# Decay attention: 22 instead of 26 tiles of maxima ahead of the first step, and each set of maxima sent in two transfers, the first ahead of the second group's packed rows

## The chip, the cores and the metric

The kernel runs on one core of one Trainium2 chip. The metric is the device time of one execution in microseconds. A core has TensorE (PE in the profile, its weight loads PEld), VectorE (DVE), ScalarE (ACT), GpSimd (POOL) and SyncE (SP), which here issues all DMAs.

## The reference, cut to what matters

The program is a chain of eight residual blocks on 2 batches of 1024 tokens by 128 features; the activation is kept transposed, 128 features on the partitions and 2048 tokens along the free axis, in chunks of 512. The change touches the fifth block alone, the decay attention, between two normalizations:

```
q = x @ W_q; k = x @ W_k; v = x @ W_v
latent_kv = (k + v) @ W_down_kv
k_rec, v_rec = latent_kv @ W_up_k, latent_kv @ W_up_v      # 16 heads of 8 features
scores = einsum('bhqd,bhkd->bhqk', qh, k_rec) / sqrt(128)
scores = scores * exp(-0.01 * |i - j|)                     # decay, before the softmax
out = einsum('bhqk,bhkd->bhqd', softmax(scores), v_rec)
x = x + out @ W_o
```

There are 2 batches of 16 heads, each with scores of 1024 x 1024. The softmax subtracts the exact row maximum, so that the maximum of each query's decayed scores has to be known before the exponential of that query is taken.

## The kernel before, in words

The heads go through in eight groups of four (n = 0 to 7; groups 0 to 3 are batch 0). For every group the queries and keys, split into bf16 pieces of 48 rows, are brought from a scratch tensor in HBM into packed rows in SBUF (`packs(n)`, L1290, eight transfers of 192 KB), with two more rows (KP and KP + 1) for the maxima.

Two kinds of work run over these rows.

*Maxima.* A unit `u` (256 in all, 32 in a group) is one head and 128 queries: TensorE makes 128 x 1024 scores (L916), VectorE multiplies them by the decay strip and takes the maximum in one instruction (`unit_dve`, L926). When the 16 units of half a group are done, a *turn* `j` (16 of them) follows: VectorE copies the maxima (`both_sides_dve`, L942), TensorE transposes them (L935), VectorE splits them into two bf16 parts (`maxima_dve`, L949 and L951, semaphore `m_l`), and SP sends them into the packed rows (`maxima(j)`, L1299, semaphore `pk_m`), for each of two row halves and each of two parts: four transfers of 4 KB.

*Steps.* A step `T` (128 in all, 16 in a group) is 128 keys by 512 queries for four heads: scores with the maxima subtracted (L1014), on every second step also the diagonal tile, made (L981), multiplied on VectorE by the decay's correction (`fix_dve`, L1063) and finished (L994); ScalarE takes four exponentials (L1048) and on even steps a fifth for the diagonal (L1054); TensorE multiplies by the values (L1038, in two halves).

The order is written out by hand in `a1_pe`, `a1_act`, `a1_dve` and `a1_sp`. `LEAD` units run alone ahead of step 0, with a filling matmul each on TensorE (`idle_pe`, L1117). Then each step carries two units, until none are left; that is so for steps 0 to 114 with LEAD = 26. Turn j stands in step `maxima_at(j)` = 8j - (LEAD - 16)/2, that is 8j - 5; its maxima are needed by step 8j, where TensorE waits for `pk_m`. The steps after the last unit carry the output projections (`PROJ_PE`, L1080, float32, chunk c and quarter a of the heads) of chunks 0 to 2 and the first part of the next normalization (`LN5_AT`: center L1395 at the end of that step, variance L1402 two steps later, its scale four steps later on VectorE). Chunk 3 is projected after the last step.

The queue of SP has its own written order: the stores of the split pieces (L1283), `packs(0)`, the rest of the stores, `packs(1)`, the first maxima, `packs(2)`, the second maxima and so on. Later, for each group: the denominators go out (L1304, L1308), the odd maxima, the packed rows of group n + 4 (n = 0 to 3), the reciprocals (L1312, L1317), the even maxima. When the reciprocals have landed, GpSimd normalizes the group (`normalize`, L877).

Of the kernel before, what the change touches and what calls it, by code (L numbers as in the profile page):

```python
# [20 lines left out]
P = 128  # L21
# [17 lines left out]
NKT = S // P  # L39
LAMBDA = 0.01  # L40
KP = 48
# [63 lines left out]
def build(nc, W, out):  # L105

    ctx = ExitStack()
    with ctx:
        def sb(name, shape, dt=F32):
            return ctx.enter_context(nc.sbuf_tensor(name, shape, dt))  # L110
# [3 lines left out]
        def sem(name):  # L114
            if name not in sems:
                sems[name] = ctx.enter_context(nc.semaphore(name))
            return sems[name]
# [576 lines left out]
        NSLOT = 4  # L694
        PK = place([NSLOT * 2, 2, 4, CH], BF16).rearrange("p (n e) f a t -> p n e f a t", e=2)
# [15 lines left out]
        MH = sb("MH", [P, 2, 2, P], BF16)  # L711
# [10 lines left out]
        a1_stored = sem("a1_stored_even"), sem("a1_stored_odd")  # L722
        pk_in = [[sem(f"pk_in{sl}{sub}") for sub in range(2)] for sl in range(NSLOT)]
        pk_m, p1_s, p1_free = sem("pk_m"), sem("p1_s"), sem("p1_free")
# [12 lines left out]
        STORES = 16 * 4 * 3  # L737
        NSTEP, NUNIT = NGRP * NS, NGRP * NT1
        NTH, KH = NT1 // 2, NKT // 2
        LEAD = NTH + 10  # L740
        S_BANKS, D_BANK, O_BANK = (0, 1, 4, 5), 2, 3
        RING = (NUNIT - LEAD) // 2 + 1
        HEADS = (0, 2, 1, 3)
# [16 lines left out]
        def is_diag(T):  # L760
            return T % 2 == 0
# [128 lines left out]
        def maxima_at(j):  # L890

            return NKT * j - (LEAD - NTH) // 2

# [49 lines left out]

        def maxima_dve(v, j):
            if j >= 2:
                v.wait_ge(pk_m, 64 * (j - 1))
            v.wait_ge(m_t, j + 1)
            rows = slice(0, 2 * NTH)
            v.tensor_copy(MH[rows, j % 2, 0, :], PS[rows, D_BANK, 0:P]).then_inc(m_h, 1)  # L949
            v.wait_ge(m_h, j + 1)  # L950
            v.tensor_tensor(MH[rows, j % 2, 1, :], PS[rows, D_BANK, 0:P], MH[rows, j % 2, 0, :],  # L951
                            ALU.subtract).then_inc(m_l, 1)
# [149 lines left out]
        def a1_residual_dve(v, c):  # L1102
# [3 lines left out]

        TURNS = {maxima_at(j): j for j in range(1, 2 * NGRP)}
        PROJ_FROM = (NUNIT - LEAD) // 2 + 1
        PROJ_PE = {PROJ_FROM: ((0, 0), (0, 1)), PROJ_FROM + 1: ((0, 2), (0, 3)), PROJ_FROM + 2: ((1, 0), (1, 1)),
                   PROJ_FROM + 3: ((1, 2), (1, 3)), NSTEP - 4: ((2, 0), (2, 1)), NSTEP - 3: ((2, 2),), NSTEP - 1: ((2, 3),)}  # L1110
        LAST_SUMS, LN5_AT, SIXTH_FREE = NSTEP - 4, NSTEP - 9, NSTEP - 4
        RECIPROCAL_AT = 6

        def idle_pe(t, times, bank):

            for _ in range(times):
                t.matmul(PS[:, bank, 0:2 * P], ident[:], w1T[:, 0:2 * P], start=True, stop=True)  # L1117

        def a1_pe(t):
            a1_prep_pe(t)  # L1120
            idle_pe(t, 18, 7)
            t.wait_ge(a1_v, 1 + NCH)
            for u in range(LEAD):
                unit_pe(t, u, 0)
                unit_pe(t, u, 1)
                idle_pe(t, 1, O_BANK)
                if u == NTH + 1:
                    maxima_pe(t, 0)
            diag_pe(t, 0, HEADS[0:2])
            diag_pe(t, 0, HEADS[2:4])  # L1130
            t.wait_ge(a1_neg, 2)
            for T in range(NSTEP):
                n, s = divmod(T, NS)
                u = LEAD + 2 * T
                turn = TURNS.get(T)

                def unit(k, half):
                    if u < NUNIT:
                        unit_pe(t, u + k, half)

                def diag(heads):
                    if is_diag(T):
                        diag_max_pe(t, T, heads)
                    elif T + 1 < NSTEP:
                        diag_pe(t, T + 1, heads)
                if s % NKT == 0:
                    t.wait_ge(pk_m, 64 * (T // NKT + 1))
                if s == 0:
                    t.wait_ge(vg_in, n + 1)
                after_turn = T - 1 in TURNS  # L1150

                def block(heads):
                    if after_turn:
                        diag_pe(t, T, heads)
                    elif turn is None:
                        diag(heads)
                scores_pe(t, T, 0)
                unit(0, 0)
                block(HEADS[0:2])
                scores_pe(t, T, 1)  # L1160
                unit(0, 1)
                if T >= RING:
                    scores_pe(t, T, 2)
                    scores_pe(t, T, 3)
                    block(HEADS[2:4])
                if T == SIXTH_FREE:
                    t.wait_ge(ln_free, 1 + late_count(LN5[0], 1))
                if T == PROJ_FROM:
                    t.wait_ge(p1_free, NUNIT)
                for c, a in PROJ_PE.get(T, ()):  # L1170
                    project_pe(t, c, a)
                if T > 0:
                    pv_pe(t, T - 1, 0)
                if T < RING:
                    scores_pe(t, T, 2)
                unit(1, 0)
                if T < RING:
                    block(HEADS[2:4])
                if turn is not None:
                    maxima_pe(t, turn)  # L1180
                if T < RING:
                    scores_pe(t, T, 3)
                unit(1, 1)
                if T > 0:
                    pv_pe(t, T - 1, 1)
                if after_turn:
                    diag_max_pe(t, T, HEADS[0:2])
                    diag_max_pe(t, T, HEADS[2:4])
                if T == LN5_AT:
                    t.wait_ge(x_ready, 1 + NCH * 4 + 2)  # L1190
                    center_pe(t, LN5[0], 0, 6, XR)
                if T == LN5_AT + 2:
                    variance_pe(t, LN5[0], 0, 6)
                if T == LAST_SUMS:
                    last_sums_pe(t, 2)
            pv_pe(t, NSTEP - 1, 0)
            pv_pe(t, NSTEP - 1, 1)
            last_sums_pe(t, 3)
            project_pe(t, 3, 0)
            project_pe(t, 3, 1)  # L1200
            project_pe(t, 3, 2)
            project_pe(t, 3, LAST)
# [24 lines left out]
        def a1_dve(v):  # L1227
            a1_prep_dve(v)
            for u in range(LEAD):
                unit_dve(v, u)  # L1230
# [5 lines left out]
            for T in range(NSTEP):  # L1236
# [14 lines left out]
                if s == RECIPROCAL_AT and n > 0:  # L1251
                    v.wait_ge(den_in, 16 * n)
                    v.reciprocal(RS, RS).then_inc(den_r, 1)
                for c, a in PROJ_PE.get(T, ()):
                    if a == LAST and c < 2:
# [11 lines left out]
        def a1_sp(sp):  # L1267
# [3 lines left out]
            def stores(c):  # L1271
                b, j = c // 2, c % 2
                for k in range(3):
                    for v in range(4):
                        rows = PIECE_ROWS[v // 2][k]
                        if k == 0:
                            sp.wait_ge(a1_hi, 4 * c + v + 1)
                        elif k == 1:
                            sp.wait_ge(a1_mid, 4 * c + v + 1)
                        else:  # L1280
                            sp.wait_ge(a1_lo_free, 8 + 4 * c + v + 1)
                        dst = scr[v // 2, b, :, rows, j, v % 2, :]
                        sp.dma_start(dst, SPL[c % 2][:, v, k:k + 1, :].broadcast_to((P, 3 - k, CH))  # L1283
                                     ).then_inc(a1_stored[c % 2], 16)

            def packs(n):
                for g in (1, 0, 3, 2):
                    for side in range(2):
                        dst = PK[row0(g):row0(g) + KP, n % NSLOT, side, :, g // 2 * 2:g // 2 * 2 + 2, :].rearrange("p f v t -> p f (v t)")
                        sp.dma_start(dst, scr_heads[side, n, g]).then_inc(pk_in[n % NSLOT][g // 2], 16)  # L1290

            def maxima(j):
                sp.wait_ge(m_l, j + 1)
                n, hf = divmod(j, 2)
                for half in range(2):
                    for k in range(2):
                        row = 64 * half + KP + k
                        dst = PK[row:row + 1, n % NSLOT, 0, hf, :, :].rearrange("p a (t q) -> p (a t) q", q=P)
                        sp.dma_start(dst, MH[NTH * half:NTH * half + NTH, j % 2, k, :]).then_inc(pk_m, 16)  # L1299

            def denominators(n):
                sp.wait_ge(o_free, 2 * n + 2)
# [22 lines left out]
            packs(0)  # L1325
            stores(2)
            stores(3)
            packs(1)
            sp.wait_ge(a1_stored[0], 2 * STORES)
            sp.wait_ge(a1_stored[1], 2 * STORES)  # L1330
            maxima(0)
            packs(2)
            maxima(1)
            packs(3)
# [1052 lines left out]
```

## Time and profile before

| | us |
|---|---|
| median of 3 runs | 1121.29 (1120.91 to 1122.62) |
| the profiled execution's own time | 1125.32 |
| its span | 1123.5 |
| stretch of the lead units | 278 to 309 |
| stretch of the 128 steps | 309 to 679 |

The profiled execution's span is what the rows below are cut from. In a row of the timeline the first number is the start in us from the span's start, the second the time until the last of the merged instructions ended; then the engine, the line, the operation, what is written and read, and how many; in brackets the idle time of the engine ahead of it and what ended that. Step numbers don't stand in the trace: they are counted from the diagonal exponential (L1054), one on each even step.

### The profile page before, as it was taken

What the parts mean: (1) busy time and instruction counts of PE and PEld (TensorE: products, weight loads), DVE (VectorE), ACT (ScalarE), POOL (GpSimd) and SP (SyncE); (2) the same over time, 40 slices, a digit from 0 to 9 for tenths busy, and PEclk for the clock granted to TensorE, in tenths of its full rate; (3) what the DMA queues carried; (4) which work ended last, traced back from release to release, by engine and by line L of the source; (5) the groups of instructions that cost most, each with busy time, mean ns of one, the idle gap of its engine ahead of it and who ended that gap; (6) DMA issues with size and microseconds to landing.
All of it is one profiled execution on the core that took longest, in us unless ns stands there. A gap on an engine that the chain in (4) does not pass through costs nothing.

```text
span 1123.5 us, 15969 instructions
## 1 busy us (share of the span) xinstructions
PE 1041.1 (93%) x6036; PEld 413.5 (37%) x6048; DVE 743.8 (66%) x1194; ACT 678.7 (60%) x1140; POOL 170.5 (15%) x119
## 2 busy tenths in 40 slices
PE   5799998988999999999999989999989988999998
PEld 2233333335433333333333334443333333334443
DVE  2787326348989999999999621126879898881110
ACT  4687525446078788888888774467556656634331
POOL 0222531006000000000000000000333342340000
PEclk9899999999989999999999999999989999999999
DMA  8000000038950321303000000000000000000000
GB/s 270 1 2 1 1 0 1 0 123 233 303 90 4 64 43 23 65 4 63 9 3 8 7 2 1 1 1 0 1 0 1 0 1 0 1 10 1 10 9 10
DMA packets 31203, 38.37 MB, mean 34 GB/s; under 512 B 7964, under 2 KB 22300, under 8 KB 30744
## 3 DMA queue, kind: packets, MB, share of 16 engines
q1 hardware_dynamic: 31128, 37.37, 13.2%
q8 instruction: 48, 0.79, 0.3%
q14 instruction: 27, 0.22, 0.1%
HBM read 23.23 MB, written 13.86 MB: 33 GB/s over the span
## 4 chain that ended last, share of the span: by engine, by line
PE 51%; DVE 23%; ACT 6%; issue 2%; another core or an unknown queue 1%; DVEq 0%; ACTq 0%
PE PS L1510 17%; DVE ffn L926 15%; PE PS L1038 6%; PE PS L1014 4%; DVE PS L1063 2%; PE PS L1495 2%; PE PS L1498 2%; PE PS L1521 2%; ACT arena L1048 2%; PE PS L1577 1%; PE PS L1080 1%; PE PS L1687 1%; PE PS L916 1%; DVE arena L1724 1%; PE PS L1677 1%
## 5 line engine op out<-in xcount | busy, mean ns | idle before, releaser
L1048 ACT ACTIVATE arena<-PS 128x384 f32<-128x384 f32 (+1 forms) x512 | 258.0, 547 | 84.4 <-PE PS L1014 72.9
L926 DVE CUSTOM_DVE_ANT_0 ffn<-PS,XP 128x1024 bf16<-128x1024 f32 x256 | 300.7, 1216 | 4.4 <-PE PS L916 4.4
L916 PE MATMUL PS<-arena 48*128 48x512 bf16 (+3 forms) x704 | 173.6, 325 | 5.6 <-DVE MX L926 5.5
L1014 PE MATMUL PS<-arena 50*128 50x512 bf16 (+3 forms) x640 | 169.4, 320 | 1.6 <-ACT arena L1048 1.3
L1038 PE MATMUL PS<-arena 128*32 128x256 f32 x2048 | 162.4, 393 | 1.0
L1540 ACT ACTIVATE arena<-PS,w_scl 128x512 f32<-128x512 f32 x64 | 43.5, 687 | 139.5 <-PE PS L1510 139.2
L1510 PE MATMUL PS<-arena,w_h2T 128*128 128x512 f32 x256 | 118.0, 607 | 0.0
L1510 PE MATMUL PS<-arena,w_h1T 128*128 128x512 f32 x256 | 115.3, 594 | 0.4 <-DVE arena L1549 0.4
L1014 PEld LDWEIGHTS PS<-arena 50*128 50x128 bf16 x640 | 50.4, 94 | 101.9 <-ACT arena L1048 70.2
L1724 DVE TENSOR_TENSOR_SCAN arena<-arena 128x512 f32<-128x512 f32 x64 | 81.4, 1273 | 0.3
L1510 PEld LDWEIGHTS PS<-arena,w_h2T 128*128 128x128 f32 x256 | 49.6, 195 | 61.1 <-issue 58.6
L1510 PEld LDWEIGHTS PS<-arena,w_h1T 128*128 128x128 f32 x256 | 48.2, 190 | 60.6 <-issue 55.5
L1038 PEld LDWEIGHTS PS<-arena 128*32 128x32 f32 x2048 | 42.1, 108 | 66.0 <-issue 54.3
L1063 DVE TENSOR_TENSOR PS<-PS,w_fixT 128x512 f32<-128x512 f32 x64 | 44.5, 696 | 32.5 <-PE PS L981 32.5
L1555 DVE SCALAR_TENSOR_TENSOR XR<-PS,w_scl,XR 128x512 f32<-128x512 f32 x8 | 6.0, 747 | 83.7 <-PE PS L1521 83.7
L1715 DVE TENSOR_TENSOR arena<-arena,PS 128x512 f32<-128x512 f32 x64 | 42.8, 669 | 25.9 <-PE PS L1671 13.5
L916 PEld LDWEIGHTS PS<-arena 48*128 48x128 bf16 x704 | 50.7, 93 | 24.9 <-DVE MX L926 12.6
L1760 POOL TENSOR_TENSOR arena<-arena 128x512 f32<-128x512 f32 x32 | 40.6, 1271 | 112.6 <-DVE arena L1724 112.6
L1533 ACT ACTIVATE arena<-PS,w_scl 128x512 f32<-128x512 f32 x32 | 22.0, 687 | 49.0 <-PE PS L1495 47.9
L503 DVE TENSOR_TENSOR arena<-arena 128x896 f32<-128x896 f32 (+1 forms) x40 | 43.9, 1137 | 8.6 <-ACT arena L444 8.2
L1054 ACT ACTIVATE arena<-PS 128x512 f32<-128x512 f32 x64 | 38.7, 605 | 12.4 <-PE PS L994 12.4
L877 POOL TENSOR_TENSOR arena<-arena 128x1024 f32<-128x1024 f32 x7 | 16.6, 2370 | 191.5 <-DMA arena<-rscr 191.5
(228 smaller groups left out, 1558.0 us busy)
## 6 DMA issues: line engine op xcount, KB each, us to landing
arena<-scr SPq DMA_DIRECT2D x64, 192.0 KB, 5.7
scr<-arena SPq DMA_DIRECT2D x16, 384.0 KB, 5.5
scr<-arena SPq DMA_DIRECT2D x16, 256.0 KB, 4.9
scr<-arena SPq DMA_DIRECT2D x16, 128.0 KB, 3.3
XP<-xT SPq DMA_DIRECT2D x1, 1024.0 KB, 4.9
w_h1T<-h1T SPq DMA_DIRECT2D x1, 1024.0 KB, 6.7
w_h2T<-h2T SPq DMA_DIRECT2D x1, 1024.0 KB, 8.6
arena<-MH SPq DMA_DIRECT2D x64, 4.0 KB, 1.7
```

The source lines that it names most:

```text
L503: v.tensor_tensor(e, e, window, ALU.mult).then_inc(a0_masked, 1)
L916: mm = t.matmul(PS[:, bank, k0 - lo:k1 - lo], packed(m, g, v, slice(q * P, (q + 1) * P), KP), packed(m, g, 2 + v, slice(k0, k1), KP), star ...
L926: v.tensor_tensor_reduce(JUNK[:, u % 2, :], PS[:, bank:bank + 2, :].rearrange("p a b -> p (a b)"), STRIP[:, at:at + S], 1.0, -3.0e38, ALU. ...
L1014: mm = t.matmul(PS[:, score_bank(T, i), at:at + b_ - a_], packed(n, g, 2 + v, slice(kt * P, (kt + 1) * P), KP + MROWS), packed(n, g, v, sl ...
L1038: mm = t.matmul(PS[32 * g:32 * g + 32, O_BANK, q:q + b_ - a_], VG[:, n % 2, kt, g, :], PT[:, T % 2, g, a_:b_], start=(s % NKT == 0), stop= ...
L1048: nc.scalar.activation(PT[:, T % 2, score_head(T, i), a0_:a1_], PS[:, score_bank(T, i), a0_:a1_], ACT.Exp).then_inc(s_free, 1)
L1063: v.tensor_tensor(PS[:, D_BANK, :], PS[:, D_BANK, :], fixT[:], ALU.mult).then_inc(dg_fix, 1)
L1510: mm = t.matmul(PS[:, ring_bank(i, 8 + q), :], (h1T, h2T)[layer][:, kk * HID1 + blk * P:kk * HID1 + (blk + 1) * P], f1_hidden(i, layer)[:, ...
L1540: nc.scalar.activation(f1_hidden(i, 1 - layer)[:, blk, :], PS[:, ring_bank(i, 8 + q), :], ACT.Gelu, scale=scl[:, s0 + blk:s0 + blk + 1]).t ...
L1715: v.tensor_tensor(DBX[:, u % 2, :], DU[:, chunk(c)], PS[:, B_BANK, :], ALU.mult).then_inc(m_dbx, 1)
L1724: v.tensor_tensor_scan(h, h, DBX[:, u % 2, :], 0.0 if c % 2 == 0 else HL[:, n:n + 1], ALU.mult, ALU.add).then_inc(m_st, 1)
L1760: nc.gpsimd.tensor_tensor(s[2 * i], s[2 * i], s[2 * i + 1], ALU.add).then_inc(m_pair, 1)
```

## The change

`LEAD` goes from 26 to 22, so the turns stand in steps 8j - 3, units last until step 116, and the steps without units are 117 to 127 with the projections dealt out anew. `maxima(j)` sends both row halves in one transfer: two transfers of 32 pieces of 256 bytes to two partitions rather than four of 16 pieces to one. The first maxima go out before `packs(1)`.

```
-        LEAD = NTH + 10
+        LEAD = NTH + 6
@@ maxima_dve
-                v.wait_ge(pk_m, 64 * (j - 1))
+                v.wait_ge(pk_m, 32 * (j - 1))
@@ projections and the next normalization
-        PROJ_PE = {PROJ_FROM: ((0, 0), (0, 1)), PROJ_FROM + 1: ((0, 2), (0, 3)), PROJ_FROM + 2: ((1, 0), (1, 1)),
-                   PROJ_FROM + 3: ((1, 2), (1, 3)), NSTEP - 4: ((2, 0), (2, 1)), NSTEP - 3: ((2, 2),), NSTEP - 1: ((2, 3),)}
-        LAST_SUMS, LN5_AT, SIXTH_FREE = NSTEP - 4, NSTEP - 9, NSTEP - 4
+        PROJ_PE = {PROJ_FROM: ((0, 0), (0, 1), (0, 2)), PROJ_FROM + 1: ((0, 3), (1, 0), (1, 1)), PROJ_FROM + 2: ((1, 2), (1, 3)),
+                   NSTEP - 3: ((2, 0), (2, 1)), NSTEP - 2: ((2, 2),), NSTEP - 1: ((2, 3),)}
+        LAST_SUMS, LN5_AT, SIXTH_FREE = NSTEP - 4, NSTEP - 8, NSTEP - 3
@@ a1_pe
-                    t.wait_ge(pk_m, 64 * (T // NKT + 1))
+                    t.wait_ge(pk_m, 32 * (T // NKT + 1))
@@ maxima
-                for half in range(2):
-                    for k in range(2):
-                        row = 64 * half + KP + k
-                        dst = PK[row:row + 1, n % NSLOT, 0, hf, :, :].rearrange("p a (t q) -> p (a t) q", q=P)
-                        sp.dma_start(dst, MH[NTH * half:NTH * half + NTH, j % 2, k, :]).then_inc(pk_m, 16)
+                for k in range(2):
+                    dst = PK[KP + k:KP + k + 65:64, n % NSLOT, 0, hf, :, :].rearrange("p a (t q) -> p (a t) q", q=P)
+                    src = MH[0:2 * NTH, j % 2, k, :]
+                    sp.dma_start(dst, src).then_inc(pk_m, 16)
@@ the queue of SP
             stores(3)
+            sp.wait_ge(a1_stored[0], 2 * STORES)
+            maxima(0)
             packs(1)
-            sp.wait_ge(a1_stored[0], 2 * STORES)
             sp.wait_ge(a1_stored[1], 2 * STORES)
-            maxima(0)
             packs(2)
```

`PROJ_FROM` is computed from LEAD: it was step 116 and is step 118.

## Rows read from the trace of the kernel before

**Rows 1.** The page: busy time of each engine in us (share of the span), instructions.

```profile
PE 1041.1 (93%) x6036; PEld 413.5 (37%) x6048; DVE 743.8 (66%) x1194; ACT 678.7 (60%) x1140; POOL 170.5 (15%) x119
```

**Rows 2.** Windows: length, PE, PEld, DVE, ACT, POOL busy (x count), PEclk, DMA, GB/s.

```profile
314.00:320.00 6.00, 6.00 (x52) 2.18 (x49) 4.16 (x8) 3.54 (x7) 0.00 (x0) 0.58 0.05 9
...
358.00:403.00 45.00, 42.59 (x498) 15.72 (x490) 43.86 (x80) 36.88 (x75) 2.77 (x2) 1.00 0.24 42
...
630.00:650.00 20.00, 19.36 (x163) 7.89 (x159) 6.87 (x15) 12.17 (x26) 2.36 (x1) 1.00 0.04 10
```

**Rows 3.** Timeline, VectorE, at the last lead units and the first maxima's end.

```profile
299.60 0.28 DVE L951 TENSOR_TENSOR MH<-PS,MH 32x128 bf16<-32x128 f32 x1
...
304.38 1.21 DVE L926 CUSTOM_DVE_ANT_0 ffn<-PS,XP 128x1024 bf16<-128x1024 f32 x1
...
308.96 0.68 DVE L1063 TENSOR_TENSOR PS<-PS,w_fixT 128x512 f32<-128x512 f32 x1
```

**Rows 4.** Timeline, TensorE, scores of step 0.

```profile
308.99 0.32 PE L1014 MATMUL PS<-arena 50*128 50x384 bf16 x1 [0.29 <-issue]
```

**Rows 5.** Timeline, SP's queue: maxima and packed rows.

```profile
300.51 2.45 SPq L1299 DMA_DIRECT2D arena<-MH  x4
...
322.26 2.42 SPq L1299 DMA_DIRECT2D arena<-MH  x4
...
366.46 2.41 SPq L1299 DMA_DIRECT2D arena<-MH  x4
368.92 5.07 SPq L1290 DMA_DIRECT2D arena<-scr  x8
```

**Rows 6.** Line L1299, issue to landing: first maxima, then the second.

```profile
DMA to landing us min/median/max: 5.9/6.2/6.5
...
DMA to landing us min/median/max: 1.6/1.7/1.7
```

**Rows 7.** The page, DMA issues: packed rows, KB each, us to landing.

```profile
arena<-scr SPq DMA_DIRECT2D x64, 192.0 KB, 5.7
```

**Rows 8.** Timeline, VectorE and GpSimd, at turns in steps 11 and 27.

```profile
342.51 0.18 DVE L942 COPY MXD<-MX 128x32 f32<-128x32 f32 x1
...
385.26 2.37 POOL L877 TENSOR_TENSOR arena<-arena 128x1024 f32<-128x1024 f32 x1 [26.50 <-DMA arena<-rscr]
386.84 0.82 DVE L942 COPY MXD<-MX 128x32 f32<-128x32 f32 x1
```

**Rows 9.** Line L942 in steps 43 and 75: ns min/median/max, start.

```profile
L942 DVE COPY MXD<-MX x1: 828/828/828, 431.8 to 431.8; 128x32 f32<-128x32 f32 x1
...
L942 DVE COPY MXD<-MX x1: 673/673/673, 521.2 to 521.2; 128x32 f32<-128x32 f32 x1
```

**Rows 10.** Timeline, ScalarE: diagonal exponentials of steps 0, 2, 112 and 114.

```profile
311.48 0.59 ACT L1054 ACTIVATE arena<-PS 128x512 f32<-128x512 f32 x1
...
319.50 0.59 ACT L1054 ACTIVATE arena<-PS 128x512 f32<-128x512 f32 x1
...
625.90 0.60 ACT L1054 ACTIVATE arena<-PS 128x512 f32<-128x512 f32 x1
...
631.28 0.60 ACT L1054 ACTIVATE arena<-PS 128x512 f32<-128x512 f32 x1
```

**Rows 11.** Timeline, TensorE, steps without units.

```profile
633.85 0.34 PE L1014 MATMUL PS<-arena 50*128 50x128 bf16 x2
...
643.10 1.98 PE L1080 MATMUL PS<-arena,w_wo 128*128 128x512 f32 x4
...
646.79 1.98 PE L1080 MATMUL PS<-arena,w_wo 128*128 128x512 f32 x4
...
649.71 1.98 PE L1395 MATMUL PS<-XR,w_center 128*128 128x512 f32 x4
...
665.35 2.87 PE L1080 MATMUL PS<-arena,w_wo 128*128 128x512 f32 x4
...
676.60 2.08 PE L1038 MATMUL PS<-arena 128*32 128x256 f32 x32
```

## The prediction

> **What bounds the kernel now.** I read the page first, then the windows over the attention, then the timeline of each engine at its two ends. The page has TensorE busy for 93% of the span [rows 1], but that is an average over stages, and the change touches one. The windows split the attention in three. In the stretch of steps with units VectorE is busy 43.86 of 45 us, TensorE 42.59 and ScalarE 36.88 [rows 2]: VectorE sets the pace (a matmul's end is modelled, VectorE's isn't). In the lead, units follow each other on VectorE at (308.96 - 304.38) / 4 = 1.145 us with nothing else of the attention beside them [rows 3]. In the steps without units VectorE is busy 6.87 of 20 us, TensorE 19.36, ScalarE 12.17 [rows 2]: TensorE sets the pace, because of float32 projections. So one quantity decides: 256 units and their fixes are a fixed load on VectorE, and what matters is how many steps run beside them and how many are left for the end.
>
> **Four units fewer in the lead.** They go from 304.38 to 308.96 on VectorE, 4.58 us [rows 3]. Step 0's scores began at 308.99, right behind the last [rows 4], so they could begin at 304.4: -4.58, if the maxima have landed by then.
>
> **Have they?** This is where the old order was tight. The four transfers were issued from 300.51 to 302.96 [rows 5] and took 5.9 to 6.5 us to land [rows 6], since `packs(1)` stood ahead of them; the last issue, near 302.4, plus 5.9 to 6.5 is 308.3 to 308.9, just ahead of 308.99. With 22 units and that order, step 0 would wait until 308.9 and all of the 4.58 would be lost. In the new order `packs(1)` (eight transfers, 5.07 us to issue such a set [rows 5]) goes behind. The maxima themselves don't come earlier, as they follow unit 17; SP sent them at 300.51 because it was then free, and `m_l` was set at 299.60 + 0.28, near 299.9 [rows 3]. Two issues of 0.6 us (2.45 / 4 [rows 5]) put the last at 300.5; landing 1.7 us later, as for maxima with an empty queue [rows 6], gives 302.2, and 2.2 us are spare. Bounds: at 5.7 us, the row of packed transfers [rows 7], it is 306.2 and costs 1.8; at 1.7 nothing. I take nothing: both are SBUF to SBUF and 4 to 8 KB, so the 1.7 row is nearest; the stores in front were issued five us earlier. The price on the other side: `packs(1)` is issued 301.1 to 306.2 rather than ahead of 300.5, so it lands by 306.2 + 8, some 314. It is first read by unit 32, now in step 5, after 320. Nothing waits. `packs(2)` moves by the same 3 us and is needed 40 us on.
>
> **Fewer, larger transfers.** After every turn TensorE's next wait for `pk_m` is now three steps, not five, behind it, with `m_l` late in the turn's step: two whole steps are left. Two steps with units took 631.28 - 625.90 = 5.38 us [rows 10]. The last of two issues goes out 0.6 us after `m_l` (0.02 us passed between `m_l` and the issue at 322.26), plus 1.7 is 2.3, so 3.1 us are spare. With four transfers it would have been 1.8 + 1.7 = 3.5: that fits too, so the merging of halves matters little here. What a transfer to two partitions takes no row shows; between 1.7 and 5.7 us [rows 6, 7] I take 2, and note that the wait decides only above 5.38 - 0.6 = 4.8 us.
>
> The Trainium skill speaks against this edit: "DMA: Bandwidth & Descriptors" (section on why a DMA increments its semaphore by 16) has the number of DMA engines used by one transfer as the largest number up to 16 that divides the slowest dimension of both sides. By that the old transfer (16 pieces each side) ran on 16 engines and the new one (2 partitions against 32) runs on 2, with 16 pieces in a row on each. No row here shows such a transfer. By that rule the landing gets longer by 15 pieces on one engine; how much is open, and it moves the sum only if it passes the 4.8 us above.
>
> **Two more steps with units, two fewer without.** Two steps with units cost 5.38 us [rows 10], and step 118 takes the part of 116 (it follows the last turn in both). Scores of step 116 began at 633.85 [rows 11]; the new 118 begins at 633.85 - 4.58 + 5.38 = 634.65, +0.80.
>
> From there to the next normalization's center: before, four steps with two projections each, 649.71 - 633.85 = 15.86 us. Now three steps with three, three and two. The eight projections stay. What goes is one step's other work: the last of these steps took from 643.10 to 646.79, 3.69 us, of which two projections are 1.98; the rest is 1.7 [rows 11]. -1.7, wholly on TensorE, which is the bound there.
>
> From the center on: before, eight steps to the end of step 127's values, 676.60 + 2.08 - 649.71 = 28.97 us. Now seven. Here ScalarE holds the middle (exponentials, squares, table load and roots), and one step of it is 36.88 / 45 x 5.38 / 2 = 2.2 [rows 2, 10]; after that TensorE, with four projections that stay. This stretch also has TensorE's clock at half: two projections took 2.87 at 665.35 rather than 1.98 [rows 11]. Following each engine's order by hand, I get 27.3 us if that dip comes again and 25.4 if not: -1.7 to -3.6. I take -2.2. The last sums of chunk 2 wait for the normalization's scale, which is four steps behind the center as before, now in the same step; by hand it is done 1 us ahead of them.
>
> **A stall that goes.** The turns in steps 27, 43 and 75 have a copy of the maxima of 0.82, 0.83 and 0.67 us instead of 0.18 [rows 8, 9]: GpSimd's normalization of the group, 385.26 to 387.63, runs over it, and the copy ends only near the end of that. Beyond 0.18 they are 0.64 + 0.65 + 0.49 = 1.78 us on VectorE, the bound. Where will the two stand? From the issue of the maxima at 366.46 the chain is: maxima 2.4, packed rows from 368.92, reciprocals behind those packed rows, normalization at 385.26: 18.8 later; the next turn's copy at 386.84: 20.4 later [rows 5, 8]. The turns move by two steps against the reciprocal (which stays in step 22), but the packed rows are tied to the maxima ahead of them and hold the reciprocals' transfers back. Two issues fewer take 1.2 from the chain: normalization at 17.6 to 20.0, copy at 20.4. It is clear by 0.4 us. I take all of the 1.78; the bounds are 0 and -1.78.
>
> What VectorE waits after each turn for the diagonal tile stays: the units and the columns in that step are the same.
>
> **Sum.** -4.58 + 5.38 - 1.7 - 2.2 - 1.78 = -4.88, on the span 1123.5 and the own time 1125.32 of the profiled execution: 1120.4. The median of the runs shown is 4.0 below that own time, and taken from it the forecast is 1116.4 us.
>
> **Rivals.** *A, the stall stays* or comes back at other turns: the normalization ends only 0.4 us ahead of the copy, and SP's order ties the two. Then -3.1: 1118.2. For it speaks the small margin; against it that both ends hang on one transfer of SP's queue, so that their distance varies little. *B, the clock.* After step 0 TensorE's granted clock fell from 2.4 GHz to its lower level, 1.2: 0.58 on average over 314 to 320 [rows 2]. Before it fell TensorE was waiting in step 0 and 1 for exponentials and the fix. That start is the same now, only 4.6 us earlier. Diagonal exponentials of steps 0 to 2 are 8.0 us apart where 5.38 is usual [rows 10], so a dip costs up to 2.6. If it and the late dip stay away, 2.6 + 1.4 more: 1112.4; if one more comes or one lasts twice as long: 1119.0. *C, slower: late maxima at every turn.* If a transfer to two partitions takes 6 to 6.5 us (as behind other transfers [rows 6]), each of 15 turns loses 0.6 + 6.25 - 5.38 = 1.5 us on TensorE, VectorE then stands still with it, 22 us, less the 4.9 gained: 1138. The stall begins at 4.8 us landing; break-even is at 4.8 + 4.9 / 15 = 5.1 us. Against it: at other turns nothing is in the queue. *D, no gain:* step 0 waits for something else (the stores' completion, which SP now awaits ahead of the first maxima, up to 4.6 us later) and the four units' time is lost: 1121.0. The wait is for chunk 2's stores; chunk 3's were all issued behind them, by 295.4, so it should be over.
>
> **Numbers.** The forecast as it stands 0.50; A 0.20; B 0.16 (half on each side); D 0.09; C 0.05. Of the forecast's and A's spread by the end of the steps (-1.7 to -3.6) most lies below 1119. The range that leaves no more than 2 in 10 out is 1113.5 to 1119.4. 0.2% is about what this kernel's measurement tells from no change: faster is below 1119.05: 0.82; within, 0.12; slower, above 1123.5: 0.06.
>
> **What would show it.** Right: scores of step 0 near 304.4; the first maxima landing in about 2 us; turns' copies all 0.18; step 118's scores near 632.9 (634.65 less 1.78); center near 647.0; the end of step 127's values near 673.8. The prediction is wrong if TensorE waits for `pk_m` at steps 8j, if the copies still take 0.8, or if ScalarE's lag after the table load makes the last seven steps as long as the eight.

## The result, and the profile after

| | before | after |
|---|---|---|
| median, us (14 executions each) | 1123.67 (1120.00 to 1128.14) | 1118.45 (1117.57 to 1125.56) |
| ratio | | 0.9955, 95% interval 0.9939 to 0.9972 |
| profiled execution, own time | 1125.32 | 1123.12 |
| its span | 1123.5 | 1121.3 |

The change makes the kernel 0.45% faster, 5.1 us of 1123.67, with an interval from 3.1 to 6.9. The forecast was 4.88 us off the time of before: 1116.4, with a range from 1113.5 to 1119.4, from a median of before of 1121.29. The median of before stands 2.4 us higher here, and that of after 2.0 above the forecast. Repeated later beside other kernels, the changed kernel stood at 0.9967 (0.9946 to 0.9988). So the size is right. The trace shows that a term which the prediction put at nothing is 2.2 us, and that the median holds something which none of the five terms is.

One of the twelve executions of the kernel with the diagonal tile put behind the unit (below, under "The new wait taken away") took 1458.32 us at a mean granted clock of 0.649; the 1115.50 us and the ratio given for that kernel leave it out, and its median with all twelve is 1117.34.

The profiled execution of the changed kernel is one of its slower ones: 1123.12, where 10 of 14 lie at or below 1119.23. Against that of before it shows only 2.2 us. What the difference holds, TensorE's granted clock above all, is taken up under "The end" and with the prediction.

The page after, as [rows 1]:

```profile
span 1121.3 us, 15933 instructions
PE 1037.8 (93%) x6040; PEld 410.3 (37%) x6040; DVE 742.6 (66%) x1194; ACT 679.3 (61%) x1140; POOL 170.7 (15%) x119
```

**The start.** SP's queue, as [rows 5], and TensorE's scores of step 0, as [rows 4]. The maxima go out at 300.16, the packed rows of groups 1 and 2 behind them, and the scores begin at 304.05, not 308.99: -4.94. Of this 0.56 us is given back at once: the first diagonal exponential comes 3.05 us behind the scores (307.10, below) and came 2.49 behind them before [rows 4, 10].

```profile
300.16 1.23 SPq L1298 DMA_DIRECT2D arena<-MH  x2
301.43 10.19 SPq L1290 DMA_DIRECT2D arena<-scr  x16
```

```profile
304.05 0.32 PE L1014 MATMUL PS<-arena 50*128 50x384 bf16 x1
```

**The transfers.** For a merged transfer the trace gives no landing. Two other rows stand in. First the counts of packets, before and after:

```profile
DMA packets 31203, 38.37 MB, mean 34 GB/s; under 512 B 7964, under 2 KB 22300, under 8 KB 30744
```

```profile
DMA packets 30242, 38.35 MB, mean 34 GB/s; under 512 B 7004, under 2 KB 21340, under 8 KB 29784
```

There are 960 small packets fewer. 64 transfers of 16 pieces with 16 completions each are 2048 packets; 32 transfers of 32 pieces with 2 completions each are 1088; the difference is 960. Then the second turn's two transfers, issued from 323.12 to 324.25, in windows of half a us (columns as in [rows 2]): the DMA engines are silent until 324.0, they move the 16 KB of the two transfers by 325.5, and the next packed rows begin after that.

```profile
323.50:324.00 0.50, 0.50 (x11) 0.16 (x8) 0.50 (x1) 0.47 (x2) 0.00 (x0) 1.00 0.00 0
324.00:324.50 0.50, 0.50 (x13) 0.31 (x7) 0.23 (x2) 0.20 (x1) 0.00 (x0) 1.00 0.06 15
324.50:325.00 0.50, 0.50 (x11) 0.16 (x8) 0.27 (x1) 0.46 (x2) 0.00 (x0) 1.00 0.05 10
325.00:325.50 0.50, 0.47 (x9) 0.02 (x2) 0.50 (x2) 0.41 (x2) 0.00 (x0) 1.00 0.04 8
325.50:326.00 0.50, 0.44 (x5) 0.20 (x5) 0.50 (x1) 0.00 (x0) 0.00 (x0) 1.00 0.85 106
```

In windows of a tenth of a us there are two bursts, 324.2 to 324.6 and 324.8 to 325.2, for issues at 323.12 and some 0.57 later: the pieces have moved by 1.5 us after their issue. The same windows on the kernel before have the first of the four transfers, issued at 322.26, over by 323.6, 1.3 to 1.4 us after its issue, and it is landed by 1.7 [rows 6]. A merged transfer is thus some 0.1 us longer, at twice the bytes. When its completion lands is not in the trace; 1.8 us is an estimate from these numbers.

**The stall of the copies.** Line L942 after, ns min/median/max of all 16, as [rows 8, 9]. Not one copy is over 0.182 us. The normalization of group 0 runs from 383.70 to 386.08, and the copy of that turn comes at 388.19:

```profile
L942 DVE COPY MXD<-MX x16: 180/181/182, 297.1 to 633.9; 128x32 f32<-128x32 f32 x16
```

```profile
383.70 2.38 POOL L877 TENSOR_TENSOR arena<-arena 128x1024 f32<-128x1024 f32 x1 [29.15 <-DMA arena<-rscr]
```

**The loop.** ScalarE's diagonal exponentials of steps 0, 8, 16 and 112 after, as [rows 10]. From step 0 to step 112 it is 314.86 us; before it was 625.90 - 311.48 = 314.42. Three stalls of 1.78 us together are gone, and the loop is 0.44 us longer. (Steps 0 to 2 are 0.39 shorter in it, 7.63 us and 8.02 before; from step 8 to 112 it is 290.37 against 289.92, +0.45.)

```profile
307.10 0.59 ACT L1054 ACTIVATE arena<-PS 128x512 f32<-128x512 f32 x1
...
331.59 0.60 ACT L1054 ACTIVATE arena<-PS 128x512 f32<-128x512 f32 x1
...
353.82 0.60 ACT L1054 ACTIVATE arena<-PS 128x512 f32<-128x512 f32 x1
...
621.96 0.60 ACT L1054 ACTIVATE arena<-PS 128x512 f32<-128x512 f32 x1
```

Steps 8 to 16 took 353.82 - 331.59 = 22.23 us; before, in the same view:

```profile
335.98 0.60 ACT L1054 ACTIVATE arena<-PS 128x512 f32<-128x512 f32 x1
...
358.07 0.60 ACT L1054 ACTIVATE arena<-PS 128x512 f32<-128x512 f32 x1
```

22.09 us. What TensorE waits for in the loop (engine, line, waited for; us in total, times, longest), before (358 to 619) and after (354 to 615):

```profile
PE PS L916 <- DVE MX L926: 4.7, 12, 0.4
PE PS L935 <- DVE MXD L942: 1.3, 3, 0.5
PE PS L981 <- DVE MH L951: 0.6, 3, 0.2
```

```profile
PE PS L916 <- DVE MX L926: 4.4, 11, 0.4
PE PS L981 <- ACT arena L1054: 3.0, 12, 0.2
PE PS L994 <- DVE PS L1063: 1.3, 6, 0.2
PE PS L1014 <- ACT arena L1048: 0.2, 1, 0.2
```

The three waits for the stalled copies are gone, and twelve new ones have come: the diagonal tile's matmul (L981) waits 0.25 us for the diagonal exponential of the step before it. (The six waits at L994 are new too; they are still there when the twelve are taken away below, so they cost nothing that shows.) On VectorE it is seen in step 11 of the changed kernel: where units follow each other without a gap, the one at 338.21 begins 0.21 us late.

```profile
336.86 1.22 DVE L926 CUSTOM_DVE_ANT_0 ffn<-PS,XP 128x1024 bf16<-128x1024 f32 x1
338.00 0.08 DVE L926 DVE_READ_ACCUMULATOR2_ANT MX<- 128x1 f32 x1
338.21 1.22 DVE L926 CUSTOM_DVE_ANT_0 ffn<-PS,XP 128x1024 bf16<-128x1024 f32 x1
...
342.24 1.22 DVE L926 CUSTOM_DVE_ANT_0 ffn<-PS,XP 128x1024 bf16<-128x1024 f32 x1
343.39 0.08 DVE L926 DVE_READ_ACCUMULATOR2_ANT MX<- 128x1 f32 x1
343.50 0.18 DVE L942 COPY MXD<-MX 128x32 f32<-128x32 f32 x1
```

The last of these rows is the copy of the turn in step 13. It follows the last unit that it needs, and begins 0.11 us behind the 343.39 at which a unit would have begun.

**The end.** TensorE after, as [rows 11]: step 118's first scores, the center, and the last values.

```profile
635.28 0.33 PE L1014 MATMUL PS<-arena 50*128 50x384 bf16 x1
...
649.16 1.98 PE L1394 MATMUL PS<-XR,w_center 128*128 128x512 f32 x4
...
675.29 2.08 PE L1038 MATMUL PS<-arena 128*32 128x256 f32 x32
```

| stretch of the profiled executions | before | after | difference | forecast |
|---|---|---|---|---|
| start of step 0's scores | 308.99 | 304.05 | -4.94 | -4.58 |
| step 0 to the first step behind the last turn | 324.86 | 331.23 | +6.37 | +3.60 (5.38 - 1.78) |
| from there to the center | 15.86 | 13.88 | -1.98 | -1.7 |
| center to the last values | 28.97 | 28.21 | -0.76 | -2.2 |

The second row is 0.44 in the loop to step 112, 0.56 ahead of the first diagonal exponential, and 5.37 from step 112 on, where the two more steps with units are.

The last row has the clock in it. Windows after (columns as in [rows 2]): 0.51 of the full clock, which is 1.2 GHz, from 306.8 to 313.6, and 0.50 from 661.6 to 668.4. The columns of the second fence are the same, for the kernel before: there 1.2 GHz held for half as long, from 663.8 to 667.1, in which the slow projections of [rows 11] stand. The span is 0.9 us shorter still behind these stretches, where nothing was changed.

```profile
306.80:313.60 6.80, 6.78 (x47) 1.94 (x48) 5.26 (x10) 4.14 (x8) 0.00 (x0) 0.51 1.07 182
...
655.00:661.60 6.60, 5.40 (x52) 2.12 (x44) 1.99 (x3) 6.42 (x10) 0.00 (x0) 1.00 0.00 0
661.60:668.40 6.80, 6.65 (x33) 2.50 (x32) 0.64 (x2) 4.06 (x10) 0.00 (x0) 0.50 0.00 0
```

```profile
663.80:667.10 3.30, 3.30 (x22) 1.56 (x15) 1.23 (x3) 2.71 (x7) 0.00 (x0) 0.50 0.00 0
667.20:676.00 8.80, 8.80 (x76) 3.38 (x75) 1.29 (x2) 5.60 (x13) 0.00 (x0) 1.00 0.01 2
```

### The profile page after: what moved, and what is told of

Read it like the earlier page. It is cut to its first block, busy times and chain, and to the rows that moved or that the text cites. A ratio compares the mean times of both kernels' runs of the same rounds, so it can differ in the third digit from the quotient of the medians.

```text
span 1121.3 us, 15933 instructions
## 1 busy us (share of the span) xinstructions
PE 1037.8 (93%) x6040; PEld 410.3 (37%) x6040; DVE 742.6 (66%) x1194; ACT 679.3 (61%) x1140; POOL 170.7 (15%) x119
## 4 chain that ended last, share of the span: by engine, by line
PE 59%; DVE 13%; ACT 9%; issue 2%; DVEq 0%; ACTq 0%
PE PS L1509 17%; PE PS L1038 9%; DVE ffn L926 6%; PE PS L1014 6%; ACT arena L1048 3%; PE PS L1494 2%; PE PS L1520 2%; PE PS L916 2%; PE PS L1497 2%; DVE PS L1063 2%; PE PS L1576 1%; PE PS L1080 1%; PE PS L1686 1%; ACT arena L1054 1%; PE PS L981 1%
## 5 line engine op out<-in xcount | busy, mean ns | idle before, releaser
L1063 DVE TENSOR_TENSOR PS<-PS,w_fixT 128x512 f32<-128x512 f32 x64 | 44.5, 696 | 27.3 <-PE PS L981 27.3
L1054 ACT ACTIVATE arena<-PS 128x512 f32<-128x512 f32 x64 | 38.7, 605 | 13.4 <-PE PS L994 13.4
```

The lines of the kernel that those rows point to most:

```text
L1054: nc.scalar.activation(PT[:, T % 2, :, at:at + P], PS[:, D_BANK, :].rearrange("p (g q) -> p g q", g=GH), ACT.Exp).then_inc(dg_free, 1)
L1063: v.tensor_tensor(PS[:, D_BANK, :], PS[:, D_BANK, :], fixT[:], ALU.mult).then_inc(dg_fix, 1)
```

## The experiments

All ratios are against the kernel before, run beside it on the same chip. At some 1120 us the interval is 2 to 3 us to either side; so each verdict rests on rows where it can.

**The order in SP's queue alone taken back.**

```
-            sp.wait_ge(a1_stored[0], 2 * STORES)
-            maxima(0)
             packs(1)
+            sp.wait_ge(a1_stored[0], 2 * STORES)
             sp.wait_ge(a1_stored[1], 2 * STORES)
+            maxima(0)
```

> The changed kernel, but packs(1) again ahead of the first maxima. Theory (order): the two transfers of the first maxima are issued near 300.5 and 301.1, land 6 to 6.5 us later behind the packed rows, near 307.5, and step 0's scores begin near 307.5 instead of 304.05: 3.4 us slower than the changed kernel, about 1.3 us faster than before. Rival (merging, not order, made the room): two transfers land in about 2 us wherever they stand, scores at 304.1, no loss.

Measured: 1122.31 us, ratio 1.0001 (0.9980 to 1.0021). TensorE had its diagonal tiles at 303.55 and then stood still until the maxima were there:

```profile
306.58 0.47 PE L1014 MATMUL PS<-arena 50*128 50x384 bf16 x1 [2.40 <-issue]
```

That is 2.5 us later than in the changed kernel, not 3.4. The profile names no releaser ("issue"), since a merged transfer has no landing in it; that it is the maxima rests on the edit, which changes nothing else. At the start 2.4 of the 4.9 us remain, yet the median has no gain: only 4 of these 12 executions had a granted clock of 0.985 or more. So the order is worth half of what the start gains; merging the transfers does not replace it.

**The merging alone taken back.** Four transfers in `maxima` as before, with 64 in place of 32 in the three waits' factors.

> The changed kernel, but four transfers for each set of maxima, as before. Theory: no TensorE wait at steps 8j (last issue 1.8 us after the maxima are ready, 1.7 to land, 5.4 us available), but GpSimd's normalization starts 1.2 us later against the turn and three or four of the copies of the maxima take 0.7 to 0.8 us again instead of 0.18: 1.5 to 2 us slower than the changed kernel. Rival: the merging is worth nothing and all copies stay at 0.18: the same as the changed kernel within 0.3 us.

Measured: 1119.71 us, ratio 0.9979 (0.9958 to 1.0000). In its profile one copy stalls, not three or four:

```profile
520.98 2.36 POOL L877 TENSOR_TENSOR arena<-arena 128x1024 f32<-128x1024 f32 x1 [32.10 <-DMA arena<-rscr]
522.53 0.86 DVE L942 COPY MXD<-MX 128x32 f32<-128x32 f32 x1
```

For the other three groups the normalization ended 0.74, 0.33 and 0.15 us ahead of the copy. In the changed kernel these distances are 2.11, 1.54, 1.17 and 1.17. From step 8 to step 112 it is 291.04 us against 290.37: +0.67, the one stall. So the direction of the theory holds and its size doesn't: the merging is worth 1.0 to 2.0 us of margin, and only one group here, 0.8 us short, needed it. TensorE doesn't wait for the maxima at steps 8j here either. In the medians the two kernels can't be told apart.

**The turn's place alone.** The kernel before with one line changed.

```
-            return NKT * j - (LEAD - NTH) // 2
+            return NKT * j - 3
```

> The kernel before (26 units in the lead, four transfers, old order) with its turns in steps 8j - 3 instead of 8j - 5, nothing else. Theory (the place of the turn costs): every eight steps take 0.15 to 0.2 us more, as in the changed kernel, because after the half's copy in step 8j ScalarE is late with the diagonal exponential of step 8j + 2 and the turn in 8j + 3 no longer covers it: about 2.3 us slower than before, with TensorE waiting at L981 for L1054 some 14 times by 0.2. Rival: the place costs nothing and the loss in the changed kernel comes from the fewer lead units (VectorE less far ahead): same as before within 0.3 us.

Measured: 1123.91 us, ratio 1.0001 (0.9978 to 1.0024), an interval from -2.5 to +2.7 us, which holds both the theory's +2.3 and the rival's 0. TensorE's waits in the same stretch:

```profile
PE PS L916 <- DVE MX L926: 4.3, 11, 0.4
PE PS L981 <- ACT arena L1054: 3.0, 12, 0.3
PE PS L994 <- DVE PS L1063: 1.3, 6, 0.2
```

With 26 units in the lead the same twelve waits for L1054 are there: they come from the place of the turn, not from the shorter lead. The loop grew by less, though: from the turn's maxima to the next turn's copy it is 20.79 us here, 20.69 before and 20.90 in the changed kernel. VectorE shows why:

```profile
340.43 1.22 DVE L926 CUSTOM_DVE_ANT_0 ffn<-PS,XP 128x1024 bf16<-128x1024 f32 x1
...
341.79 1.22 DVE L926 CUSTOM_DVE_ANT_0 ffn<-PS,XP 128x1024 bf16<-128x1024 f32 x1
...
345.83 1.22 DVE L926 CUSTOM_DVE_ANT_0 ffn<-PS,XP 128x1024 bf16<-128x1024 f32 x1
...
346.97 0.17 DVE L942 COPY MXD<-MX 128x32 f32<-128x32 f32 x1
```

The unit in step 11 begins 1.36 us behind the one ahead of it, where 1.14 or 1.15 is usual: 0.21 late, as in the changed kernel. So the place costs the whole 0.21 here too. But the copy begins 1.14 us behind the unit ahead of it, without the 0.11 us that it loses in the changed kernel, because with 26 units in the lead and this place the turn no longer follows its own last unit. That gives back half. And the three stalls of the copies went too (longest 0.227 us), with four transfers: moving the turn by two steps is enough for that. From step 8 to step 112 it is 288.82 us.

**SP's two edits alone, on the kernel before** (the two diffs of SP from the change, LEAD 26).

> The kernel before with the two edits of SP's queue alone (first maxima ahead of packs(1), two transfers), 26 units in the lead. Theory: scores of step 0 stay at 309, as the units bind them; the first maxima land in about 2 us near 302.5; GpSimd's normalization comes 1.2 us earlier, the copies in steps 27, 43 and 75 fall from 0.8 to 0.18: 1.8 us faster than before. Rival: the copies' stall is not from the normalization and stays: the same as before within 0.3 us.

Measured: 1119.90 us, ratio 0.9979 (0.9958 to 1.0000). The three stalls are gone, the longest copy takes 0.251 us:

```profile
L942 DVE COPY MXD<-MX x16: 180/181/251, 297.1 to 630.0; 128x32 f32<-128x32 f32 x16
```

From step 8 to step 112 it took 288.16 us instead of 289.92: -1.76 where -1.78 was expected. The stall was the normalization's, and two transfers fewer ahead of it remove it. This run is also the loop with the turns at their old place and no stall: the changed kernel's 290.37 is 2.21 us more.

**The new wait taken away.** In the changed kernel, in steps 8j + 3, the unit's second half is put ahead of the diagonal tile:

```
+                behind = T < RING and T % NKT == 3
                 scores_pe(t, T, 0)
                 unit(0, 0)
-                block(HEADS[0:2])
+                if not behind:
+                    block(HEADS[0:2])
                 scores_pe(t, T, 1)
                 unit(0, 1)
+                if behind:
+                    block(HEADS[0:2])
```

> The changed kernel, with one order turned round in steps 8j + 3: TensorE makes the second half of the unit's scores before it waits for the diagonal exponential of step 8j + 2. Theory (TensorE's 0.2 us wait at L981 for L1054 holds back the unit and so VectorE): VectorE's gap ahead of that unit goes, eight steps fall from 22.25 to 22.1 us, 2 us over the 14 half groups. Rival: the wait is only moved to the fix behind it, and nothing changes.

Measured: 1115.50 us, ratio 0.9943 (0.9918 to 0.9967); the changed kernel beside it, which was run again:

> The changed kernel itself, once more, beside the three below. Theory: 0.9955 of before again, within 0.002; loop of eight steps 22.25 us without a reciprocal in it (22.1 before), no copy of the maxima over 0.3 us. The place and length of the stretches at 1.2 GHz vary from execution to execution and move the time by some us either way.

gave 1118.74 us, ratio 0.9967 (0.9946 to 0.9988). The intervals overlap; the rows don't. The waits for L1054 at L981 are gone from TensorE's list, and steps 8 to 16 take 22.02 us:

```profile
332.23 0.60 ACT L1054 ACTIVATE arena<-PS 128x512 f32<-128x512 f32 x1
...
354.25 0.60 ACT L1054 ACTIVATE arena<-PS 128x512 f32<-128x512 f32 x1
```

From step 8 to step 112 it is 287.62 us against 290.37 and 290.38 in the two profiles of the changed kernel: -2.75, where 2 were expected. The gap of 0.21 us 13 times is 2.7.

**The clock at the start.** Four filling matmuls in step 0.

```
                 unit(0, 0)
+                if T == 0:
+                    idle_pe(t, 2, O_BANK)
                 block(HEADS[0:2])
+                if T == 0:
+                    idle_pe(t, 1, O_BANK)
...
+                if T == 0:
+                    idle_pe(t, 1, O_BANK)
                 unit(1, 1)
```

> The changed kernel, with four filling matmuls (128 x 256 float32) in step 0, where TensorE waits 0.87 us for the first fix and 0.36 us for exponentials. Theory (TensorE's waits in step 0 bring the clock down to 1.2 GHz from about 306 to 313): the clock stays at 2.4 GHz and step 0's diagonal exponential to step 2's falls from 7.6 to about 5.6 us, 2 us faster than the changed kernel. Rival: the later steps 1 and 2 bring it down, or the filling matmuls delay the scores, and the same 7.6 us remain.

Measured: 1118.85 us, ratio 0.9964 (0.9946 to 0.9983). In the profile TensorE's clock stays at 2.4 GHz through the stretch in which the changed kernel has 0.51:

```profile
306.80:313.60 6.80, 6.35 (x68) 2.44 (x68) 6.23 (x12) 5.58 (x13) 0.00 (x0) 1.00 1.08 168
```

From step 0's diagonal exponential to step 2's it is 5.68 us instead of 7.63, but the first comes 3.91 us behind the scores of step 0, not 3.05, because of the filling: 1.1 us net where 2 were expected, and the median does not show it. All 12 executions had a granted clock of 0.985 or more.

**Both of the last two together**

> The changed kernel with both of the edits above. Theory: they add, 4 us faster than the changed kernel, 0.992 of before. Rival: one or both do nothing.

Measured: 1114.02 us, ratio 0.9927 (0.9904 to 0.9950), the fastest kernel of this study: 8.2 us under the median of before beside it, 4.7 under the changed kernel's, where 4 were expected. From step 8 to step 112 it is 287.62 us, from step 0 to step 2 5.68, each as with its edit alone, and the profile has no stretch at 1.2 GHz at either end of the steps.

**Why ScalarE is late in step 8j + 3.** Each half's sums copied twice, after and before:

```
+            nc.scalar.copy(ON[:, n, hf * CH:(hf + 1) * CH], PS[:, O_BANK, :]).then_inc(a1_twice, 1)
+            a.wait_ge(a1_twice, 2 * n + hf + 1)
             nc.scalar.copy(ON[:, n, hf * CH:(hf + 1) * CH], PS[:, O_BANK, :]).then_inc(o_free, 1)
```

> The changed kernel, with ScalarE's copy of each half's sums (L1059, 0.6 us) made twice in a row. Theory (after this copy ScalarE is late with the diagonal exponential of step 8j + 2, and TensorE waits for that in step 8j + 3): TensorE's wait there grows from 0.2 to 0.6 us or more, and eight steps take 0.4 to 0.5 us more than the changed kernel's 22.25. Rival (the wait has nothing to do with the copy): 22.25 again.

> The kernel before, with the same copy made twice. Theory (there the turn stands in step 8j + 3, TensorE makes the next diagonal tile one step later, and the lateness is covered): eight steps grow by at most 0.2 us from 22.1, less than half of what the changed kernel loses. Rival: the copy costs the same 0.4 to 0.5 us in both.

Measured: 1130.90 us, ratio 1.0060 (1.0033 to 1.0087), and 1132.09 us, ratio 1.0068 (1.0041 to 1.0095). Both theories missed; the rival that the copy costs the same in both holds, at another size. Eight steps grew by about 0.6 us in both, in the pair right behind the copy, and by a wait that neither theory named; TensorE's longest group of waits in the one and in the other is the same (380 to 600, L1039 is the values' matmul, L1062 the second copy):

```profile
PE PS L1039 <- ACT arena L1062: 6.9, 10, 0.7
```

The values of the next half wait for this copy to free their bank, so that doubling it holds TensorE back first, and TensorE's wait for the diagonal exponential stays at 0.3. The test does not reach its question: that the copy makes ScalarE late remains argued, not shown. It does show that each copy more is paid at its full length.

**The clock and the start's place.** The changed kernel with 29 filling matmuls ahead of the lead instead of 18.

> The changed kernel, with 29 filling matmuls instead of 18 ahead of the lead units, so that all that follows starts some 4.6 us later, about where it stood in the kernel before. Theory (the higher granted clock of the changed kernel's executions, 0.985 or more in 19 of 26 against 27 of 67 before, comes from when its idle spots fall): that share drops to about 4 in 10 and the median is 6 to 7 us above the changed kernel's. Rival (it comes from the change's own work, or is chance): the share stays at 7 in 10 and the median is 4.6 above.

Measured: 1124.10 us, ratio 1.0004 (0.9986 to 1.0022); step 0's scores at 308.82. 11 of 12 executions have a granted clock of 0.985, one 0.982; none has the 0.986 to 0.988 of most executions of the changed kernel, and none falls to 0.98. The median is 5.4 us above that of the repeated run, with 4.8 of shift. Neither expectation fits: the share did not fall to 4 in 10. But the 11 more filling matmuls, or the later place of all that follows them, do change which clock an execution gets. This profile has no stretch at 1.2 GHz behind the center (its only one around the steps is from 310.0 to 317.0), so it shows the end without one: 676.80 + 2.08 - 653.58 = 25.30 us.

## Why the prediction was right, and where it wasn't

*Four units fewer, -4.58: right.* It was -4.94. Of this some 0.5 us is a wait that stood in the time of before: there the diagonal tiles began at 308.07 and the scores 0.92 us later [rows 4], after 303.61 and 0.44 us later. The landing of the first maxima near 308.9, which the prediction worked out, was already late. By the first diagonal exponential the gain is 311.48 - 307.10 = 4.38. Rival D is excluded.

*The maxima must have landed: right.* With the old order 2.5 of the 4.94 us are lost at the start, where the prediction had all of the 4.58.

*Merged transfers: right that nothing waits for them.* There is no wait for `pk_m` in the loop. The prediction weighed a rule of the Trainium skill against it ("DMA: Bandwidth & Descriptors", the section on why a DMA increments its semaphore by 16): that such a transfer runs on 2 engines rather than 16. The count of packets agrees with the rule exactly (960 fewer, which 2 completions for each transfer give). Its price here is the 0.1 us read above, against 3 us to spare. Rival C, late maxima at every turn, is excluded.

*Two steps more with units, +5.38: right.* Steps 112 to 114 took 627.35 - 621.96 = 5.39 us again.

*The stall of the copies, -1.78: right.* The margin was not 0.4 but 1.2 to 2.1 us (1.0 to 1.9 in the repeated run's profile), since the moved turn also gives time back (shown by the turn's place alone). Rival A is excluded.

*"What VectorE waits after each turn for the diagonal tile stays": this step failed.* The units and columns in the step of the turn are the same, as said, and the 0.50 us wait is. What changed is a step without a turn. A turn puts the next diagonal tile off by one step, and before that happened in steps 8j + 3, where the diagonal exponential is late; now it happens in 8j + 5, and in 8j + 3 TensorE waits 0.25 us for it, with the unit's second half behind it in the queue. The prediction named what is queued behind `pk_m` but not what the old turn had been covering. Price: 0.44 + 1.78 = 2.2 us in the profiled executions, 2.21 against the loop with the turns at their old place and no stall, and 2.75 back when the wait is taken away. The sum had this term at nothing. So the scores of step 118 began at 635.28, not near 632.9.

*The end, -1.7 and -2.2: the first right (-1.98), the second not to be judged from this pair,* with 6.8 us at 1.2 GHz in it after and half of that before. In the profile with four transfers, where the clock was low there for as long as before, it was 677.05 - 650.11 = 26.94 us: -2.0. The prediction's two values by hand were 27.3 with such a dip and 25.4 without; the profile without (the start's place) has 25.30. So this term holds.

*Why the sum is right all the same.* With the term that was missing, -4.88 + 2.2 is -2.7. The stretches of the table, with the end at an equal dip, say the same: -4.94 + 6.37 - 1.98 - 2.03 = -2.58. The medians differ by 5.2 and, in the repeat, 3.5 us. Executions at the same granted clock of 0.986 are nearer to the rows: the median of ten of before beside the repeat is 1121.02 and that of five of the changed kernel 1118.67, -2.35. This comparison is rough, though: for the kernel with the wait taken away it gives 1114.38 - 1118.67 = -4.3, where the rows have -2.75. The rest, 0.8 to 2.5 us, goes with the clock: 19 of 26 executions of the changed kernel had 0.985 or more, 27 of 67 of before. That this is the whole of the rest is argued from these counts, not shown. It is of the kind of rival B's fast side, which was given 0.08, though not at its size (1112.4); which of the two dips the faster executions are spared can't be seen, as they have no profile. So the forecast met the number by luck: an unseen loss of 2.2 us and an uncounted gain of 0.8 to 2.5 cancelled, the one against the other. Why the changed kernel more often gets the higher clock is open.

## What to carry to other kernels

An instruction that is moved takes its side effects with it: ask not only what stands at the new place, but what had been hidden at the old one. In a queue in order, put what can't be late (the next unit of the bounding engine) ahead of what waits for another engine. And when a term of 2 us is to be judged on runs that scatter by 8, read it from a stretch of the trace (here eight steps, 22.23 against 22.02, thirteen times over), and compare medians only at the same granted clock.

## What the runs showed of the hardware that was not expected

The mean granted clock of an execution goes with its time at nearly 1 us for 0.001: of 35 executions of before beside the first four experiments, the medians are 1127.2 at 0.979, 1124.4 at 0.982 and 1120.7 at 0.986; at 0.989 before had three in all the experiments (1116.6, 1118.9, 1119.7). A transfer of 32 pieces of 256 bytes to two partitions, with two completions only, has moved its pieces by 1.5 us after its issue, one of 16 pieces to one partition, with sixteen completions, by 1.3 to 1.4. A copy of 128 x 32 float32 on VectorE, 0.18 us long, that starts while a tensor_tensor of GpSimd over SBUF is under way, ends 0.03 to 0.05 us behind it: it took 0.82, 0.83, 0.67 and 0.86 us with 0.6 to 0.8 left of the other, 0.25 and 0.23 us with 0.2 left (in the two kernels with SP's edits and with the turn's place alone), and 0.18 with 0.1 left (in the profile of before at 476.8, with GpSimd until 476.9). A unit on VectorE, which reads its scores from PSUM and the strip from SBUF, lasted its usual 1.22 us under the same instruction (384.64, in the changed kernel).
